# Two graph attention layers: probabilities from a second score product, row maxima as extra rows, and new orders of work on every engine

## The reference

```
# layer 0, per graph: one head, masked score, softmax over axis 1 (n)
output = x @ weight;  q = x @ wq;  k = x @ wk
alpha = softmax(max(q k^T, 0) * (graph != 0), axis=1)
x = layernorm(x + alpha @ output)
# layer 1, per graph: 16 heads of 32
q, k, v = heads(x @ Wq + bq), heads(x @ Wk + bk), heads(x @ Wv + bv)
scores = where(mask == 0, -inf, q k^T / sqrt(32))
out = softmax(scores, axis=-1) @ v
x = layernorm(x + out @ Wo + bo)
```

## Time and profile before

| | |
|---|---|
| median of 3 runs | 2967.49 us |
| the profiled execution, its own time | 2969.42 us |
| its span | 2967.6 us |
| PE busy | 2902.2 us, 98% |
| DVE busy | 2365.3 us, 80% |
| ACT busy | 2016.6 us, 68% |
| POOL busy | 582.6 us, 20% |

### The profile page before, as it was taken

One profiled execution on the slowest core, in us unless ns is written; L12 is line 12 of the kernel. 1 busy time (PEld: TensorE's weight loads), 2 busy tenths in 40 slices (PEclk: granted clock), 3 DMA queues, 4 the chain that ended last, 5 costly groups with the idle time before them and its releaser, 6 DMA issues. The chain is left out here.

```text
span 2967.6 us, 65967 instructions
## 1 busy us (share of the span) xinstructions
PE 2902.2 (98%) x24264; PEld 1775.5 (60%) x24264; DVE 2365.3 (80%) x4627; ACT 2016.6 (68%) x6414; POOL 582.6 (20%) x1289
## 2 busy tenths in 40 slices
PE   7899999999999999999999999999999999999996
PEld 4565666656666656666666666666666666666554
DVE  4588888888888788888788888888888888888886
ACT  3476676666676766676767766767776766776665
POOL 1121122121122121121121221121221211221210
PEclk9999999999999999999999999999999999999997
DMA  3222122222122222122221122221122221222220
GB/s 121 61 72 76 43 56 73 57 76 72 37 65 61 69 76 62 40 72 54 76 76 54 48 72 54 76 76 47 51 76 54 76 76 42 57 71 59 75 53 24
DMA packets 96369, 188.06 MB, mean 63 GB/s; under 512 B 18608, under 2 KB 34992, under 8 KB 96048
## 3 DMA queue, kind: packets, MB, share of 16 engines
q1 hardware_dynamic: 96048, 183.84, 23.3%
HBM read 49.55 MB, written 33.55 MB: 28 GB/s over the span
## 5 line engine op out<-in xcount | busy, mean ns | idle before, releaser
L647 ACT ACTIVATE e<-sm,nmax 128x128 f32<-128x128 f32 x2048 | 791.1, 391 | 27.6 <-DVE nmax L776 25.6
L598 ACT ACTIVATE qk<-front,bqk 128x512 f16<-128x512 f32 x256 | 175.9, 687 | 381.6 <-PE front L429 381.6
L825 POOL TENSOR_TENSOR ln<-ln 128x1 f32<-128x1 f32 x256 | 49.0, 192 | 1890.2 <-DVE ln L804 1496.6
L647 ACT ACTIVATION_READ_ACCUMULATOR e<-sm,nmax 128x1 f32 x2048 | 391.0, 191 | 0.0
L664 DVE SCALAR_TENSOR_TENSOR pT<-pt_bank,pT 128x512 f16<-128x512 f32 x512 | 348.9, 681 | 42.6 <-ACT pT L653 42.1
L653 ACT ACTIVATE pT<-pt_bank 128x512 f16<-128x512 f32 x512 | 302.8, 591 | 103.6 <-PE pt_bank L543 101.6
L776 DVE TENSOR_REDUCE nmax<-sm 128x4 f32<-128x512 f32 x512 | 351.3, 686 | 17.7
L429 PE MATMUL fin_bank<-W_O,oT 128*128 128x512 f16 x1536 | 356.3, 382 | 1.4 <-DVE oT L664 1.4
L429 PE MATMUL front<-W_V,yT 128*128 128x512 f16 x1536 | 354.0, 380 | 0.0
L429 PE MATMUL front<-xT,W_A 128*128 128x512 f16 x1536 | 353.6, 380 | 0.3 <-DVE xT L664 0.3
L429 PE MATMUL front<-yT,W_Q 128*128 128x512 f16 x1536 | 352.2, 379 | 1.6 <-DVE yT L664 1.6
(11 more groups left out here) (111 smaller groups left out, 4482.3 us busy)
## 6 DMA issues: line engine op xcount, KB each, us to landing
q_st<-qk SPq DMA_DIRECT2D x384, 128.0 KB, 2.4
k_st<-qk SPq DMA_DIRECT2D x384, 128.0 KB, 2.4
x_sb<-in_x SPq DMA_DIRECT2D x128, 256.0 KB, 3.4
out_x<-z_sb SPq DMA_DIRECT2D x128, 256.0 KB, 2.5
adj_i<-in_adj SPq DMA_DIRECT2D x32, 256.0 KB, 4.6
y_sb<-in_L_gnn_wq SPq DMA_DIRECT2D x1, 1024.0 KB, 5.6
yb<-in_L_gnn_wk SPq DMA_DIRECT2D x1, 1024.0 KB, 8.1
x_p<-in_L_gnn_weight SPq DMA_DIRECT2D x1, 1024.0 KB, 10.5
```

What stands on the lines that cost most here:

```text
L598: i = act.activation(dst, src, ACT.Identity, bias=bias, scale=scale)
L647: act.activation(e1[:, k % 2, h, :], sm[:, k % SM_BUFS, h, :], ACT.Exp, bias=nmax[:, k % SM_BUFS, h:h + 1], accum_out=esum[:, n % 2, head: ...
L825: pool.tensor_tensor(ln[:, 8:9], ln[:, 7:8], ln[:, 8:9], ALU.add).then_inc(moments, 1)
```

## The change

The probabilities of layer 1 are no longer transposed. A second product `T` computes the scores with keys on the partitions, from the same two stacks with the operands exchanged. The row maxima are found as before from the first product `S`, written as two halves (`m_hi`, `m_lo`), transposed by one matmul (`m`), copied to `mT`, and sent by four small DMAs (`m_stack`) into rows 96 to 99 of `q_st`; `k_st` holds a constant there, so `T` comes out with the maximum taken off. ACT computes the exponential twice from the same input, once to float16 and once to float32, and POOL makes the low half. The sums come from a column of ones beside v (33 columns instead of 32). x is split first and transposed as two float16 parts. Masks are made on POOL. Each engine has a list of its own, `<` being one group of age.

```diff
+ORDER = {
+    "PE": """
+        g.3< T.7<< yT.0< S.14<< yT.1< PV.5<< fin.0<< S.15<< yT.2< PV.6<< yT.3< T.8<< v.0< q.0< PV.7<< T.9<< m.3<< k.0<
+        xT.0 T.10<< q.1< PV.8<< oT.1<< xT.1 T.11<< PV.9<< k.1< xT.2 T.12<< q.2< PV.10<< T.13<< q.3< T.14<< xT.3 k.2<
+        k.3< PV.11<< T.15<< fin.1<< t.0 S.0< adjT.0 PV.12<< PV.13<< oT.2<< S.1< t.1 S.2< t.2 S.3< t.3 S.4< fin.2<<
+        S.5< alpha.0 PV.14<< PV.15<< m.0< S.6< alpha.1 v.1< S.7< T.0< v.2< S.8< oT.3<< T.1< z.0 z.1 S.9< v.3< T.2<
+        m.1< S.10< z.2 z.3 PV.0< T.3< PV.1< S.11< fin.3<< T.4< g.0 PV.2< S.12< PV.3< T.5< g.1 m.2< T.6< g.2 S.13<
+        oT.0< PV.4<
+    """,
+    "ACT": """
+        oT.0<< exp.6<< norm0.1< yT.0< x_hi.0 norm0.2< yT.1< norm0.3< exp.7<< yT.2< x_hi.1 yT.3< x_hi.2 x_hi.3 v.0<
+        q.0< exp.8<< mT.3<< k.0< exp.9<< q.1< exp.10<< oT.1<< norm1.3<<< exp.11<< k.1< q.2< q.3< exp.12<< k.2<
+        norm1.0<< k.3< exp.13<< t.0 t.1 oT.2<< t.2 exp.14<< t.3 exp.15<< mT.0< a_exp.0 a_exp.1 a_exp.2 a_exp.3 p_hi.0
+        p_hi.1 p_hi.2 p_hi.3 v.1< exp.0< v.2< oT.3<< z.0 z.1 exp.1< v.3< mT.1< z.2 z.3 norm1.1<< norm1.2<< exp.2<
+        exp.3< exp.4< mT.2< exp.5< norm0.0
+    """,
+    "DVE": """
+        yT.2< yT.3< T.8<< smax.15<< z1.0<< m_hi.3<< m_lo.3<< v.0< T.9<< o_inv.2<< o_inv.3<< q.0< o.2<< k.0< o.3<<
+        T.10<< xT.0 q.1< z_bn.0<< xT.1 T.11<< T.12<< k.1< xT.2 z_ag.0<< oT.1<< T.13<< q.2< o_inv.4<< q.3< T.14<< xT.3
+        adj01.0 k.2< k.3< o_inv.5<< o.4<< o.5<< z1.1<< T.15<< z_bn.1<< smin.0< o_inv.6<< adjT.0 t.0 smax.0< smin.1<
+        smax.1< t.1 smin.2< oT.2<< smin.3< smax.2< smax.3< m_hi.0< t.2 o.6<< smin.4< z_ag.1<< t.3 m_lo.0< smax.4<
+        z1.2<< smin.5< smax.5< alpha.0 o_inv.7<< o.7<< smin.6< a_max.0 alpha.1 a_max.1 z_bn.2<< p_inv.0 p_invp.0
+        smax.6< p_inv.1 p_invp.1 p_lo.0 p_lo.1 T.0< p_lo.2 p_lo.3 smin.7< z_ag.2<< v.1< smax.7< smin.8< v.2< m_hi.1<
+        T.1< smin.9< z.0 m_lo.1< oT.3<< z.1 smax.8< T.2< smin.10< v.3< z.2 T.3< z.3 smax.9< smax.10< smin.11< o_inv.0<
+        smax.11< T.4< o.0< z1.3<< y.0 m_hi.2< o_inv.1< m_lo.2< y_bn.0 T.5< y_ag.0 smin.12< y.1 o.1< y_bn.1 T.6< y.2
+        y_ag.1 y_bn.2 smin.13< smax.12< y_ag.2 oT.0< y.3 y_bn.3 y_ag.3 T.7< smin.14< z_bn.3<< z_ag.3<< yT.0 yT.1
+        smax.13< smax.14< smin.15<
+    """,
+    "POOL": """
+        lo.8<<< lo.9<<< lo.10<<< ln1.0<<< lo.11<<< lo.12<<< lo.13<<< maskT.0<< lo.14<<< lo.15<<< ln1.1<<< ln1.2<<<
+        lo.0<< resid.0<< resid.1<< lo.1<< lo.2<< lo.3<< resid.2<< resid.3<< lo.4<< ln0.0< ln0.1< lo.5<< lo.6<< ln0.2<
+        ln0.3< lo.7<< maskb.0< x_lo.0 ln1.3<<< x_lo.1 x_lo.2 x_lo.3
+    """,
+    "SP": """
+        store.3<< store.0< stack.0 stack.1 m_stack.0 m_stack.1 store.1< load.0>> load.1>> load.2>> load.3>> store.2<
+        m_stack.2 load_adj.0>> m_stack.3
+    """,
+}
...
+def steps_of(engine):
     out = []
+    for word in ORDER[engine].split():
+        name = word.rstrip("<>")
+        what, k = name.split(".")
+        out.append((what, int(k), word.count("<") - word.count(">")))
     return out
+def program(engine, groups):
+    out = []
+    for p in range(-2, groups + 4):
+        for what, k, age in steps_of(engine):
+            if 0 <= p - age < groups:
+                out.append((what, k, p - age))
+    return out
...
+            for what, k, g in program("SP", groups):
+                if what == "load":
+                    wait(sp, bn0, (g - 1) * GB + k + 1)
+                    sp.dma_start(x_sb[:, k, :], x_d[g][k, :, :]).then_inc(x_loaded[k], 16)
+                elif what == "load_adj":
+                    wait(sp, adj01_ready, g)
+                    sp.dma_start(adj_i[:, :, :], adj_d[g]).then_inc(adj_loaded, 16)
+                elif what == "stack":
+                    dst, parts = ((q_st, (HI, LO, HI)), (k_st, (HI, HI, LO)))[k]
+                    for last in range(KT):
+                        wait_freed(sp, "qk"[k], last, g)
+                    if g == 0:
+                        sp.wait_ge(setup_done, SETUP)
+                    wait(sp, t_full, g * STEPS)
+                    for r in range(4):
+                        for row, part in enumerate(parts):
+                            sp.dma_start(dst[row * DH:(row + 1) * DH, r, :, :],
+                                         qk[r * DH:(r + 1) * DH, k, part, :, :]).then_inc(stacked[k], 16)
+                elif what == "m_stack":
+                    sp.wait_ge(mT_ready, g * GB + k + 1)
+                    for part in (HI, LO):
+                        for copy in range(2):
+                            row = MAXROWS + 2 * copy + part
+                            sp.dma_start(q_st[row:row + 1, :, :, k * P:(k + 1) * P],
+                                         mT[part * HEADS:(part + 1) * HEADS, k % 2, :]).then_inc(m_stacked[k], 16)
...
                 if what == "xT":
                     if k == 0:
-                        pe.wait_ge(x_loaded, count(g, 16 * GB, 16 * GB))
-                    bank = bank_for(g)
-                    for n in range(GB):
-                        mm = pe.transpose(bank[:, n * P:(n + 1) * P], x_sb[:, n, k * P:(k + 1) * P], ident[:, :])
+                        pe.wait_ge(xhi_ready, (g + 1) * GB)
+                        pe.wait_ge(xlo_ready, (g + 1) * GB)
+                    parts = bank[:, :].bitcast(F16)
+                    for part in (HI, LO):
+                        for n in range(GB):
+                            at = (part * GB + n) * P
+                            mm = pe.transpose(parts[:, at:at + P], x_p[:, part, n, k * P:(k + 1) * P], ident16[:, :])
                     mm.then_inc(f_full, 1)
...
+                elif what == "m":
+                    pe.wait_ge(m_ready, g * GB + k + 1)
+                    pe.matmul(tail[:, 0:P], nm16[:, k % 2, :], ident16[:, :], start=True, stop=True).then_inc(m_full, 1)
+                elif what == "T":
+                    n, quad = divmod(k, QUADS)
+                    if quad == 0:
+                        pe.wait_ge(m_stacked[n], (g + 1) * 64)
+                    if k == 0 and g == 0:
+                        pe.wait_ge(ones_ready, 3)
+                    wait(pe, u_ready, g * STEPS + k)
                     for h in range(4):
-                        mm = pe.transpose(pt_bank[:, h * P:(h + 1) * P], e1[:, k % 2, h, :], ident[:, :])
-                    mm.then_inc(pt_full, 1)
+                        mm = pe.matmul(t_bank[:, h * P:(h + 1) * P], k_st[0:ROWS, h, quad, n * P:(n + 1) * P],
+                                       q_st[0:ROWS, h, quad, n * P:(n + 1) * P], start=True, stop=True)
+                    mm.then_inc(t_full, 1)
...
-                        cols = slice((4 * quad + h) * DH, (4 * quad + h + 1) * DH)
-                        mm = split_product(pv_bank[:, cols], lambda p: pT[:, k % 2, p, h * P:(h + 1) * P], lambda p: v_p[:, p, n, cols], 0, 1)
+                        head = 4 * quad + h
+                        cols = slice(head % HALF * VW, head % HALF * VW + DH + 1)
+                        mm = split_product(pv_bank[half % 2][:, cols], lambda p: pT[:, k % 2, p, h * P:(h + 1) * P],
+                                           lambda p: v_p[:, p, n, head, 0:DH + 1], 0, 1)
                     mm.then_inc(pv_done, 1)
...
                 elif what == "exp":
-                    n, quad = divmod(k, QUADS)
-                    act.wait_ge(nmax_ready, count(g, STEPS, k + 1))
-                    wait(act, pt_full, count(g, STEPS, k - 1))
-                    if quad == 0:
-                        wait(act, einv_ready, count(g, GB, n - 1))
-                    for h in range(4):
-                        head = 4 * quad + h
-                        act.activation(e1[:, k % 2, h, :], sm[:, k % SM_BUFS, h, :], ACT.Exp,
-                                       bias=nmax[:, k % SM_BUFS, h:h + 1],
-                                       accum_out=esum[:, n % 2, head:head + 1]).then_inc(exp_done, 1)
-                elif what == "pT":
-                    act.wait_ge(pt_full, count(g, STEPS, k + 1))
-                    wait(act, pv_done, count(g, STEPS, k - 1))
-                    act.activation(pT[:, k % 2, HI, :], pt_bank[:, :], ACT.Copy, scale=P1_SCALE).then_inc(pthi_ready, 1)
+                    act.wait_ge(u_ready, g * STEPS + k + 1)
+                    wait(act, pv_done, g * STEPS + k - 1)
+                    src = u[:, k % 2, :, :].rearrange("p h m -> p (h m)")
+                    act.activation(pT[:, k % 2, HI, :], src, ACT.Exp, scale=SCORE_UNSCALE).then_inc(phi_ready, 1)
+                    wait(act, p_ready, g * STEPS + k - 1)
+                    act.activation(e32[:, k % 2, :], src, ACT.Exp, scale=SCORE_UNSCALE).then_inc(e_ready, 1)
...
                 elif what == "xT":
-                    front_lo(xT[:, LO, k, :], xT[:, HI, k, :], X_SCALE)
+                    dve.tensor_copy(xT[:, :, k, :], front_bank(what, k, g)[:, :].bitcast(F16).rearrange("p (a n) -> p a n", a=2)
...
+                    wait(dve, nmax_ready, g * STEPS + k - 1)
```

(115 more changed lines are left out.)

506 lines of the change are left out of this document (238 added, 268 removed), and 18 rows, old and new, of the table LATE_ATTENTION.

## The result

The changed kernel takes 3355.39 us (median of 4 runs, 3349.85 to 3362.67), the kernel before 2967.27 beside it (4 runs): ratio 1.1311, 95% interval 1.1287 to 1.1336. It is 13% slower, 3 us from the forecast of 3358.

What follows compares the result with a forecast made beforehand. PE was taken as the bound. Its 86.3 us per pass plus waits and clock (12.4, 1.6, 1.3, 0.4, 0.3) gave a period of 102.3; 122 + 3171 - 9 + 73 = 3357, forecast 3358 us, range 3180 to 3440.

Steps and rivals of the forecast that it cites:

- The wait of S.0: PE idles before each later group's S.0 until 24 stack transfers, started after T.15, land: 12.4 us per pass, bounds 11 to 14.
- the 17 us: SP's 24 stack transfers back to back, 23 issues of 0.62 to 0.63 us and a landing of 2.4: 17.0 us.
- The clock: PE's granted clock falls after the idle time, slowing the S step and t job behind it: 1.6 us per pass, 0 to 3.
- T on `m_stack`: PE's T.8 waits for m_stack.2, 1.3 us per pass, bounds 0 and 3; T.0 waits behind m.0, 0.4.
- T on DVE's `u`: Counted among other waits inside a pass, with DVE mostly 2 to 6 us ahead: 0.3 us for all.
- the 9 us that the prediction takes off: Taken off 31 periods for work missing in the first and last: fin, PV, oT of an absent group, and xT.
- PE's work falls by 3.3 per group: On PE, 16 pT steps go (7.0 us), T adds 3.5 and m 0.2: 86.3 us per pass instead of 89.65.
- (2): Rival at the stack transfers: bytes bind at 410 GB/s, S.0 waits 5.1 us, total 3132 us; chance 0.06.
- (3): Rival at S.0: not slower, transfers pass unseen behind fin.1 and t.0, the lighter PE list sets 2936 us; chance 0.08.
- (4): Rival behind the S.0 wait: clock stays low, exponential and POOL waits come due, 4 us more per pass, 3482 us; chance 0.12.
- the 2 us that were set: Sign that the forecast is right: no wait over 2 us anywhere other than before S.0.

Runs made afterwards that it cites:

- the new lists: The changed kernel with only the orders of jobs altered on all five engines, more work between T.15 and S.0: 2944.68 us, ratio 0.9929 to the kernel before.

## Why the prediction was right

**The wait of S.0.** Predicted 12.4 per pass (12.1 worked out); measured 377.7/31 = 12.2. The three things it rested on held one by one: the distance from T.15 to the first transfer (0.47 for 0.46), the length of 24 transfers with landing (1532.64 to 1549.76 = 17.1 for 17.0) and PE's work between (5.3 for 5.2). The 0.3 that the prediction added because some issues take longer was not needed: without the last pass the mean is 12.1. It was safe to take them from the first pass of the kernel before, because the same instructions meet the same queue there.

**The reason given for the 17 us was half of it.** The prediction argued from issues 0.62 us apart and gave the byte bound a rate of 410 GB/s. That step was wrong: these transfers, 32 rows of 4 KB out of one tile into another, run at 204 to 218 GB/s with the engines 90 to 97% busy, so bytes alone cost nearly as much. Nor do issues always stand 0.62 apart: with the new lists 12 of them take 8.49 us. It did no harm to the time, but it would have misled the one who repairs the kernel: two queues alone give 20 us. The Trainium skill's table (DMA: Bandwidth & Descriptors, Anatomy of one DMA), by which descriptors are cheap to emit and most of a fixed cost of 2 us is the completion, describes transfers that GpSimd issues. The prediction left that out when it set the table against the trace: the transfers here are issued by SP or ACT, and no run shows the other path. What the runs show for SP is that 4 KB land after 1.7 us, 64 KB after 2.0 and 128 KB after 2.4, so most of a landing does not go by bytes; and that an issue takes 0.6 us whatever it carries (64 KB: 7.51 us for 12, 128 KB: 7.53), so 24 of them on one queue are a bound of their own.

**The clock.** Predicted 1.6 per pass (0 to 3). After an idle time of 12 us instead of 2.93, the way from S.0 to the end of `t.1` takes 6.58 us (1549.76 to 1556.34) where the jobs cost 4.3: 2.3, and 2.2 in the mean of the passes.

**Small waits.** T on `m_stack`: predicted 1.3 + 0.4, measured 23.0/32 = 0.7, because a row of the maxima lands after 1.7 us and not after 2.4 (the 5.6 us of PE's work beside it hold four `yT` steps, where the prediction names three):
```profile
q_st<-mT SPq DMA_DIRECT2D x512, 4.0 KB, 1.7
```
T on DVE's `u`: 20.9/32 = 0.65, predicted 0.3 for all of that kind. Together these are 1.35 for 2.0. That the period still came out is luck: the clock cost about as much more as these cost less.

**The sum.** Period 101.9 (3280.61 - 122.35 over 31) for 102.3, or for 102.0 with the 9 us that the prediction takes off; first S.0 at 122.35 for 122; from it to the last one 3158.3 for 3162; from there 74.0 for 73.

**Work per engine.** The exponential was priced at 1.25 per step and takes 623 + 617 ns; POOL's low half at 1157 takes 1159:
```profile
L566 ACT ACTIVATE pT<-u 128x512 f16<-128x512 f32 x512 | 318.8, 623 | 122.4 <-PE pv_bank L355 89.3
L568 ACT ACTIVATE e<-u 128x512 f32<-128x512 f32 x512 | 315.7, 617 | 0.0
...
L790 POOL TENSOR_TENSOR pT<-e,pT 128x512 f16<-128x512 f32 x512 | 590.8, 1159 | 1457.5 <-ACT e L568 1456.3
```
Eight float16 transposes take 0.44, `PV` with 33 columns 0.30, the `xT` copy of 1024 elements 679 ns: the ends that were taken. That PE's work falls by 3.3 per group is borne out by the kernel with one stack for all groups: PE is busy for 2800.9 us there and for 2902.2 before, 3.2 per group. DVE was put at 69 us per pass and takes 72.9 (715.50 of 1000 us). Missed were the two small steps `m_hi` and `m_lo`, below, 5.6 us per pass.

**The rivals.** (2) did not come, since bytes moved at half of its 410 GB/s, but its doubt was the right one: bytes are a limit beside the issues. (3), not slower, is what the new lists bring. (4) did not come, though its sign did: it was to show as DVE above 85% busy from S.0 to T.8. In that stretch DVE is 91% busy and PE 98%:
```profile
1549.76:1605.00 55.24, 54.16 (x515) 33.96 (x515) 50.35 (x100) 29.04 (x59) 22.25 (x38) 0.95 0.10 31
```
So a busy DVE was a wrong sign of waits on PE. The longest wait elsewhere behind the first S.0 is 2.2 us, for a row of the maxima, just over the 2 us that were set.

## What to carry to other kernels

When a change makes a reader of a single buffer later, the wait that it adds is the refill time of the buffer less the work that stands in the list between the last reader and the next use; both can be read from the kernel before, and 12 us per pass lost here against 3.3 us of saved work. Before repairing a row of transfers, work out both limits, the issues per queue and the bytes over the engines, since removing one alone may show nothing. And a change that comes with new orders is two changes: with other lists the same arithmetic went from 13% slower to 0.7% faster.
